# Strassen products for gate and up in the last seven weight groups of a 4-bit FFN, block sums on VectorE and GpSimd

## What is computed

```python
Wg = dequant_nvfp4(gate_W_packed, gate_scales)      # [4096, 512]
Wu = dequant_nvfp4(up_W_packed, up_scales)          # [4096, 512]
Wd = dequant_nvfp4(down_W_packed, down_scales)      # [512, 4096]
gate = jnp.einsum('th,nh->tn', xt, Wg)
up = jnp.einsum('th,nh->tn', xt, Wu)
gelu = jnp.tanh(0.7978845608028654 * (gate + 0.044715 * gate ** 3)) * gate * 0.5 + gate * 0.5
out = jnp.einsum('tn,hn->th', gelu * up, Wd)
```

## Time and profile before

| | |
|---|---|
| runs, us | 2811.38, 2810.78, 2814.67; median 2811.38 |
| profiled execution, us | 2812.82 |
| its span, us | 2811.0 |
| mean granted TensorE clock | 0.950 |
| busy over the span | TensorE 94%, VectorE 75%, GpSimd 44%, ScalarE 41% |

### The profile page before, as it was taken

How to read it: one execution, slowest core, us unless ns; L and a number is a source line. 1 busy time by engine, 2 the same in 40 slices (tenths; PEclk the granted TensorE clock), 3 DMA queues, 4 the chain that set the end, 5 groups by cost and what they waited for, 6 DMA issues and landing times.

```text
span 2811.0 us, 32430 instructions
## 1 busy us (share of the span) xinstructions
PE 2632.4 (94%) x11088; PEld 1873.9 (67%) x11096; DVE 2119.0 (75%) x2720; ACT 1150.8 (41%) x1690; POOL 1249.9 (44%) x836
## 2 busy tenths in 40 slices
PE   7888988888898879999999999999999999999999
PEld 4443444444344337888887777888878788888887
DVE  6999999999999986643366677777877865555553
ACT  5555455555545535422254442433343422222221
POOL 3989888888889871210001023223212422222220
PEclk9988898899889879999999999999999999999999
DMA  7755645555465427221111112112111111111111
GB/s 251 221 165 141 181 135 139 157 155 140 127 181 157 136 79 265 83 83 45 49 65 68 38 45 68 38 51 64 49 41 46 46 50 48 46 53 46 53 45 68
DMA packets 152309, 275.35 MB, mean 98 GB/s; under 512 B 27344, under 2 KB 27856, under 8 KB 151632
## 3 DMA queue, kind: packets, MB, share of 16 engines
q1 hardware_dynamic: 152144, 273.27, 32.8%
HBM read 178.01 MB, written 61.34 MB: 85 GB/s over the span
## 4 chain that ended last, share of the span: by engine, by line
PE 72%; DVE 11%; ACT 7%; issue 4%; POOL 3%; DMA 2%; SPq 0%; DVEq 0%; POOLq 0%; ACTq 0%
PE ps L1722 19%; PE ps L1724 19%; PE ps L1723 19%; PE ps L1763 8%; DVE state L1347 5%; ACT ps L848 5%; PE ps L1775 4%; POOL read L1173 2%; DMA vpack<-vl 1%; DMA uraw<-y_d 1%; PE ps L1914 1%; PE ps L1888 1%; DVE drive L1338 1%; POOL wdeq L1232 0%; DVE act_o L1662 0%
## 5 line engine op out<-in xcount | busy, mean ns | idle before, releaser
L1173 POOL TENSOR_TENSOR read<-state,c_t 128x512 f32<-128x512 f32 x512 | 666.8, 1315 | 121.8 <-DVE state L1347 89.1
L1347 DVE TENSOR_TENSOR_SCAN state<-ps,drive 128x512 f32<-128x512 f32 x512 | 620.4, 1212 | 15.0 <-ACT ps L848 13.3
L1232 POOL TENSOR_TENSOR wdeq<-packed,scales 128x1024 f32<-128x1024 f16 x96 | 256.1, 2668 | 799.1 <-DVE packed L1495 799.1
L1722 PE MATMUL ps<-xh,ghi 128*128 128x512 f32 x1536 | 608.0, 396 | 0.0
L1724 PE MATMUL ps<-xh,glo 128*128 128x512 f32 x1536 | 598.5, 390 | 0.0
L1723 PE MATMUL ps<-xl,ghi 128*128 128x512 f32 x1536 | 598.3, 390 | 0.0
L848 ACT ACTIVATE ps<-ps,a_exp 128x512 f32<-128x512 f32 x512 | 338.9, 662 | 470.7 <-PE ps L1763 469.5
L1763 PE MATMUL ps<-dpack,sel 128*128 128x512 f32 x512 | 259.9, 508 | 108.0 <-DVE state L1347 106.5
L1338 DVE TENSOR_TENSOR drive<-ps,b_t 128x512 f32<-128x512 f32 x512 | 342.3, 669 | 16.4 <-PE ps L1763 15.7
L1662 DVE TENSOR_TENSOR act_o<-act_o,ps 128x512 f32<-128x512 f32 x192 | 131.7, 686 | 290.5 <-PE ps L1724 288.8
L1100 ACT ACTIVATE ahi<-act_o 128x512 fp32r<-128x512 f32 x192 | 121.4, 632 | 521.5 <-DVE act_o L1662 521.4
(11 more groups left out here) (193 smaller groups left out, 3747.6 us busy)
## 6 DMA issues: line engine op xcount, KB each, us to landing
whi<-w_d SPq DMA_DIRECT2D x63, 256.0 KB, 4.1
wlo<-w_d SPq DMA_DIRECT2D x63, 256.0 KB, 5.3
b_d<-ev SPq DMA_DIRECT2D x32, 256.0 KB
dpack<-dh SPq DMA_DIRECT2D x64, 128.0 KB, 4.0
dpack<-dl SPq DMA_DIRECT2D x64, 128.0 KB, 3.8
b_t<-b_d SPq DMA_DIRECT2D x32, 256.0 KB, 4.1
vpack<-vh SPq DMA_DIRECT2D x64, 128.0 KB, 3.6
vpack<-vl SPq DMA_DIRECT2D x64, 128.0 KB, 2.8
```

The lines of the kernel that those rows point to most:

```text
L1173: pool.tensor_tensor(read[:, n % RRING, :], state[:, n % SRING, :], c_t[:, g % 2, :], ALU.mult).then_inc(read_ready, 1)
L1232: pool.tensor_tensor(wdeq[:, :].rearrange("p (h n) -> p h n", h=2), codes, scale, ALU.mult).then_inc(deq, 1)
L1347: dve.tensor_tensor_scan(state[:, n % SRING, :], ps[:, n % 2, :], drive[:, n % DRING, :], 0.0, ALU.mult, ALU.add)\
L1722: pe.matmul(out_, w_h, x_h, start=(start and k == 0), stop=False)
```

## The change

Groups 17 to 23 (`FAST_E` = 17 on) get their own loop, written over 44 units `v` a group. Each weight tile is taken as 2x2 blocks: output blocks j = 0, 1 by halves of the feature dimension (k = 0, 1 in the code's `block_`; each half has two feature tiles); the inputs of batches 2 and 3 are the 2x2 blocks of the other operand. With A the weight blocks and X the input blocks, the seven products (Winograd's form) are

```diff
+FAST_E = ALL_E - FFN_E + 1
+M1_AT, M5_AT, M6_AT, M2_AT, M7_AT, M3_AT, M4_AT = (
+    (0, 6, 13, 20), (1, 8, 15, 22), (2, 9, 16, 23), (3, 10, 17, 24), (4, 11, 18, 25),
+    (5, 12, 19, 26), (7, 14, 21, 28))
+UNITS = 44
+OUTS = ((0, 0), (0, 1), (1, 1), (1, 0))
...
+    xp = [post(f"xp{i}", [P, 2, S], F32, X0_ + 4096 * i) for i in range(4)]
+    xd = [post(f"xd{i}", [P, 2, S], F32, XL0 + 4096 * i) for i in range(4)]
+    xdlo = [post(f"xdlo{i}", [P, 2, S], F32R, XL0 + 4096 * i) for i in range(4)]
+    xdhi = [post(f"xdhi{i}", [P, 2, S], F32R, XH0 + 4096 * i) for i in range(4)]
+    act4 = [post(f"act4{o}", [P, S], F32, X0_ + 2048 * o) for o in range(4)]
+    m1_c11 = post("m1_c11", [P, S], F32, X0_ + 8192)
+    u2_c12 = post("u2_c12", [P, S], F32, X0_ + 10240)
+    m5_c22, u3_c21 = act_o
+    wsum = post("wsum", [P, 4, 2, P], F32, X0_ + 12288)
+    shi = [post(f"shi{k}", [P, 4, 2, P], F32R, 16384 * k) for k in range(2)]
+    slo = [post(f"slo{k}", [P, 4, 2, P], F32R, 16384 * k + 8192) for k in range(2)]
...
+            def store_out(b):
+                sp.wait_ge(added, 8 * (2 * MLP_E + FFN_E * (b // 2 + 1)) - 4 + 4 * (b % 2))
+                sp.dma_start(out[:, :, cols(b)], res[:, :, cols(b)]).then_inc(stored, 16)
+            for p in range(24 * FAST_E):
+                if p == 24 * FAST_E - 21:
+                    store_out(0)
+                    store_out(1)
...
+            for T in range(6 * FAST_E + 5, ALL_T):
+                load_tile(T)
+            store_out(2)
+            store_out(3)
...
+            def sum_high(q):
+                act.wait_ge(w_summed, fast1 + q + 1)
+                if q >= 2:
+                    act.wait_ge(m3_ready, fast0 + q - 1)
+                else:
+                    act.wait_ge(stored, 32)
+                act.activation(shi[q % 2][:, :, :, :], wsum[:, :, :, :], ACT.Copy, scale=UNF16)\
+                   .then_inc(s_hi, 1)
...
+            def copy_m5(q):
+                act.wait_ge(m5_ready, fast0 + q + 1)
+                taken(q - 1, 2)
+                act.activation(m5_c22[:, :], ps[:, bank_of_unit(M5_AT, q), :], ACT.Copy)\
+                   .then_inc(m5_copied, 1)
...
+                if T > 6 * FAST_E and T % 6 in (1, 2, 3, 4):
+                    pool.wait_ge(w_summed, fast1 + fast_tile(T // 6, T % 6 - 1) + 1)
...
+            def sum_weights(T):
+                q = fast_tile(T // 6, T % 6)
+                block_ = wdeq[:, :].rearrange("p (k f j n) -> p k f j n", k=2, f=2, j=2)
+                a11, a12, a21, a22 = (block_[:, k, :, j, :] for j in range(2) for k in range(2))
+                pool.wait_ge(deq, T - MLP_T + 1)
+                if q:
+                    pool.wait_ge(s_lo, fast1 + q)
+                else:
+                    pool.wait_ge(xd_ready, xd0 + 4)
+                pair_done[0] += 2
+                pool.tensor_tensor(wsum[:, 0, :, :], a21, a22, ALU.add).then_inc(pairs_summed, 1)
+                pool.wait_ge(pairs_summed, pair_done[0] - 1)
+                pool.tensor_tensor(wsum[:, 1, :, :], wsum[:, 0, :, :], a11, ALU.subtract)\
+                    .then_inc(pairs_summed, 1)
+                pool.tensor_tensor(wsum[:, 2, :, :], a11, a21, ALU.subtract)
+                pool.wait_ge(pairs_summed, pair_done[0])
+                pool.tensor_tensor(wsum[:, 3, :, :], a12, wsum[:, 1, :, :], ALU.subtract)\
+                    .then_inc(w_summed, 1)
+            def make_u4_c22(q):
+                pool.wait_ge(m5_copied, fast0 + q + 1)
+                pool.wait_ge(u3_made, fast0 + q + 1)
+                pool.tensor_tensor(u2_c12[:, :], u2_c12[:, :], m5_c22[:, :], ALU.add).then_inc(u4_made, 1)
+                pool.wait_ge(u4_made, fast0 + q + 1)
+                pool.tensor_tensor(m5_c22[:, :], u3_c21[:, :], m5_c22[:, :], ALU.add).then_inc(c22_made, 1)
...
+            def whole_input(i):
+                kk, b = ((0, 2), (0, 3), (1, 3), (1, 2))[i]
+                pool.wait_ge(n_lo, B)
+                pool.tensor_tensor(xp[i][:, :, :], xh[b][:, 2 * kk:2 * kk + 2, :].bitcast(F32),
+                                   xl[b][:, 2 * kk:2 * kk + 2, :].bitcast(F32), ALU.add)\
+                    .then_inc(xp_ready, 1)
...
+            def sum_low(q):
+                dve.wait_ge(s_hi, fast1 + q + 1)
+                dve.scalar_tensor_tensor(out=slo[q % 2][:, :, :, :], in0=wsum[:, :, :, :], scalar=UNF16,
+                                         in1=shi[q % 2][:, :, :, :].bitcast(F32), op0=ALU.mult,
+                                         op1=ALU.subtract).then_inc(s_lo, 1)
...
+            def make_c12(q):
+                dve.wait_ge(m3_ready, fast0 + q + 1)
+                dve.wait_ge(u4_made, fast0 + q + 1)
+                dve.tensor_tensor(u2_c12[:, :], u2_c12[:, :], ps[:, bank_of_unit(M3_AT, q), :], ALU.add)\
+                   .then_inc(c12_made, 1)
...
+                dve.wait_ge(act_done, first_u(q) + o + 1)
+                dve.tensor_tensor(act4[o][:, :], act4[o][:, :], up[:, :], ALU.mult).then_inc(prod_done, 1)
...
+            for E in range(FAST_E, ALL_E):
+                for v in range(UNITS):
+                    if v == 0:
+                        add_down(E - 1, 7)
+                    for k in range(4):
+                        q = fast_tile(E, k)
+                        if v == M6_AT[k] + 1:
+                            make_u2(q)
+                        if v == M2_AT[k] + 1:
+                            make_c11(q)
+                        if v == M7_AT[k] + 1:
+                            make_u3(q)
+                        if k % 2 and v == M2_AT[k] + 1:
+                            gated(q, 0)
+                        if v == M3_AT[k] + 2:
+                            make_c12(q)
+                            if k % 2:
+                                gated(q, 1)
+                        if k % 2 and v == M3_AT[k] + 3:
+                            gated(q, 2)
+                        if v == M3_AT[k] + 3:
+                            make_c21(q)
+                        if k % 2:
+                            if v == M3_AT[k] + 3:
+                                gated(q, 3)
+                            if v == M3_AT[k] + 5:
+                                a_low(q, 2)
+                                a_low(q, 3)
+                    for k in range(7):
+                        if v == (33, 34, 35, 36, 38, 40, 42)[k]:
+                            add_down(E, k)
...
+                    if v == 9:
+                        sum_low(fast_tile(E, 2))
+                    if v == 11:
+                        w_low(6 * E + 3)
+                    if v == 13:
+                        unpack(6 * E + 4)
+                    if v == 16:
+                        sum_low(fast_tile(E, 3))
+                    if v == 17:
+                        w_low(6 * E + 4)
+                    if v == 20:
+                        unpack(6 * E + 5)
...
+            def block_product(table, q, weights, inputs):
+                (w_h, w_l), (x_h, x_l) = weights, inputs
+                return three_pass(ps[:, bank_of_unit(table, q), :],
+                                  [(w_h[f], w_l[f], x_h[f], x_l[f]) for f in range(2)])
...
+            for E in range(FAST_E, ALL_E):
+                for v in range(UNITS):
+                    for k in range(4):
+                        q, T = fast_tile(E, k), 6 * E + k
+                        if v == M1_AT[k]:
+                            pe.wait_ge(w_lo, T + 1)
+                            if q == 0:
+                                pe.wait_ge(added, 8 * FAST_E)
+                            elif k == 0:
+                                pe.wait_ge(c11_made, fast0 + q)
+                            else:
+                                pe.wait_ge(u2_made, fast0 + q)
+                            block_product(M1_AT, q, weight_block(T, 0, 0), input_block(0, 2))\
+                                .then_inc(m1_ready, 1)
...
+                        if v == M6_AT[k]:
+                            if q:
+                                pe.wait_ge(c12_made, fast0 + q)
+                            block_product(M6_AT, q, sum_block(q, 1), difference_block(1))\
+                                .then_inc(m6_ready, 1)
...
+                        if v == M3_AT[k]:
+                            pe.wait_ge(m5_copied, fast0 + q + 1)
+                            block_product(M3_AT, q, sum_block(q, 3), input_block(1, 3))\
+                                .then_inc(m3_ready, 1)
+                        if v == M4_AT[k]:
+                            pe.wait_ge(c11_made, fast0 + q + 1)
+                            block_product(M4_AT, q, weight_block(T, 1, 1), difference_block(3))\
+                                .then_inc(m4_ready, 1)
...
+                    if v == 32:
+                        pe.wait_ge(a_lo, 8 * FAST_E + 4 * (E - FAST_E) + 4)
+                        pe.wait_ge(a_lo_pool, fast1 + 4 * (E - FAST_E) + 4)
+                    if 32 <= v <= 35:
+                        down_part(E, v - 32, (2, 3))
```

(3 more changed lines are left out.)

322 lines of the change are left out of this document (306 added, 16 removed).

## The result

The changed kernel takes **2903.74 us** (median of 4 runs, 2902.11 to 2905.91); the kernel before took 2812.62 us beside it. The ratio is 1.0324, 95% interval 1.0306 to 1.0342: 3.2% slower. The profiled execution took 2904.5 us, its span 2902.7, the mean granted clock was 0.940. The forecast was 2893, with a range of 2825 to 2960.

What follows compares the result with a forecast made beforehand. TensorE's instruction count was taken as the bound. Seven groups at 530.2 against 457.0 us (+73.2), group 16 +2 and the clock's 7 gave +82 on 2812.8, 2895; the median 1.4 lower: 2893 us, range 2825 to 2960.

Steps and rivals of the forecast that it cites:

- The turns: VectorE and GpSimd alternate whole instructions on SBUF work: 29.1 us a group for VectorE, 36.8 for GpSimd.
- Some 16.5 us behind GpSimd: Part of the 76.6 us group: the time VectorE's queue loses behind GpSimd's operations, about 16.5 us.
- The price without a row: GpSimd's turn for a 256-column sum, taken as 0.60 us from a line through other rows.
- The layout by hand: VectorE's and GpSimd's queues of one fast group set against each other at the turn prices: 76.6 us a group.
- Switch: Entry into the seven fast groups, where product one waits for the last add: 1.0 us.
- The clock's term: TensorE's slow restarts at 1.2 GHz after stalls in the fast groups: 1 us a group, 7 in all.
- Perfect packing: Rival: turns packed without a gap, a fast group takes 65.9 us; 2808 to 2816 us in all; 4%.
- the two faster cases: Rivals: VectorE's order alone binds, 62.6 us a group, 2794 us, 5%; all of the 38.1 us saved, 2775, 2%.
- the floor: Sum of both engines' turns in a fast group, packed without a gap: 65.9 us.
- the ceiling: VectorE's 50.9 us and all of GpSimd's 36.8 one after the other in a fast group: 87.7 us.
- The clock's rival: Stalls lower the granted clock under 0.78 and TensorE binds the fast groups again: 2950 to 3070 us; 6%.
- Three signs: Expected: VectorE busy over 90%, TensorE's longest waits also before M4 on C11, GpSimd dequantizations over 2.65 us.

Runs made afterwards that it cites:

- e8: Changed kernel with 12 unread matmuls more before product M6 of the second, third and fourth tile of a group: 2903.1 us.
- e6: Kernel before the change, with GpSimd given the change's new operations in the last seven groups, into memory nobody reads: 2814.1 us.
- e3: Changed kernel with GpSimd's weight sums cut to 8 of 256 columns from the fourth tile of group 17 on: 2885.4 us.
- e2: Changed kernel with U4, C22 and the two activation splits of a pair moved from GpSimd to VectorE: 2882.1 us.

## Why the prediction was right

**What bounds.** Right: TensorE was the bound before, and it no longer is. e8 shows the second half: with 36 matmuls more a group, groups 18 to 23 did not get longer.

**What it removes and adds.** The counts were exact. VectorE's own work was put at 50.9 us; busy 67.3 less the loss of 15.6 is 51.7.

**The turns.** The mechanism was right and e6 shows it alone. "Some 16.5 us behind GpSimd" was 15.6. The second unpack was laid out at 5.5 us and took 5.56. The price without a row, 0.60 for the turn of a 256-column sum, was right. The turn is the time from the end of VectorE's operation to the end of the sum that waited for it; in group 20 (GpSimd, VectorE, GpSimd):

```profile
2604.39 0.75 POOL L1409 TENSOR_TENSOR wsum<-wdeq 128x256 f32<-128x256 f32 x1 [1.66 <-DVE slo L1897]
...
2605.67 0.83 DVE L1971 TENSOR_TENSOR act<-act,m_c 128x512 f32<-128x512 f32 x1
...
2605.90 1.20 POOL L1413 TENSOR_TENSOR wsum<-wdeq 128x256 f32<-128x256 f32 x1
```

The multiply ends at 2606.50 and the sum at 2607.10. The 0.75 us of the first sum, which nobody held up, is its length from start to end; a turn is some 0.14 shorter. In the same way 512 columns take 1.29 alone and 1.15 as a turn, 1024 take 2.40 and 2.26. One small reading was off: the unpack of the earlier trace rows lost 3.4 us (0.37, 2.06 and 0.98), not 3.2; nothing hangs on it.

**The layout by hand.** Counted from where VectorE leaves the last unpack of the group before, M6 of tiles two, three and four were laid at 12.6, 26.6 and 41.8. In group 20 VectorE leaves it at 2588.31, and the three start at 2600.90, 2615.00 and 2630.34: 12.6, 26.7 and 42.0. From there to the next such point it took 35.7 instead of 34.8. What the layout had wrong is TensorE's place beside VectorE: its first product started 4.3 us before that point (2583.98), not 0.9. TensorE only waits longer for it at the first M6, since VectorE's queue closes the loop. One agreement in the first tile is luck. The layout left about 1.7 us before U2 (4.35 - 0.9, less 1.14 and 0.60 for the two operations between), where VectorE would wait for TensorE; there it waited for nothing, and then 2.25 us for ScalarE's part of a weight split that the layout had ready.

**The sum.** Switch, group 17 and its clock's 1 us: forecast 75.9, measured 78.0. Groups 18 to 22: 77.6 each, measured 78.1. Group 23: 73.3, measured 73.2. So 80.2 forecast, 84.8 measured. Group 16, forecast +2, was +4.8. The five PSUM banks did not cover VectorE's lateness: TensorE waited 3.1 us there for the seventh activation split (line 1996), behind an unpack and all that the group had added before it. It then restarted slowly, with matmuls 0.43 us apart for 3 us, and as TensorE still leads in that group, the other 1.7 us are the restart. With the scatter of 2.1 this is the distance of 10 us between 82 and 91.7.

**The clock's term.** The stalls do bring slow restarts (0.50 for 5 us), as "TensorE: Matmul & The Clock Gate", section "HAM oscillation — how this bites in real kernels", in the Trainium skill has it for work that comes after a long enough wait. I charged 1 us a group for them, 7 in all. e8, with the clock at 0.98 to 1.00, is 3.7 us faster in groups 18 to 23, 0.6 a group; and 1.7 fell in group 16, where I had charged none. The size was about right, its grounds were weak: I had written that TensorE had gaps of 3 to 4.5 us in the scan stage, but its longest idle time there, from 60 to 1040 us, is 1.7. The 0.4 a group that I charged too much stood in for VectorE's waits, which were 10.4 a group and not 9.

**The rivals.** Perfect packing (65.9 a group) and the two faster cases fell with the first group: 77.7 lies between the floor of 65.9 and the ceiling of 87.7, near the 76.6 of the layout. The clock's rival needed a granted clock under 0.78; it was 0.91 to 0.96 over a group, and in e8 0.98 to 1.00 with nearly the same time.

**What would show it.** C12 before M6, the slow unpacks, the untouched PSUM operations and the clock under 1 came as said. Three signs did not. VectorE was busy 87%, not over 90. C11 (line 1932) cost TensorE 6.0 us in all, four waits of 1.5 before M4, a tenth of what C12 cost. And GpSimd's dequantizations got no slower, from 2348 to 2902:

```profile
L1396 POOL TENSOR_TENSOR wdeq<-packed,scales 128x1024 f32<-128x1024 f16 x39 | 98.5, 2527 | 78.4 <-DVE packed L1738 78.4
...
L1735 DVE TENSOR_TENSOR bits_a<-bits_a,packed 128x512 int32<-128x512 int32 x39 | 51.1, 1310 | 1.3
...
L1730 DVE TENSOR_SCALAR bits_b<-bits_a 128x512 int32<-128x512 int32 x39 | 38.3, 981 | 1.3
```

2.53 us on the mean against 2.65 in the earlier trace rows. The unpack carries half of the loss: 1.31 us on the mean for the OR and 0.98 for the mask behind it, where 0.69 and 0.42 stood.

## What to carry to other kernels

Count what a saving on TensorE adds to the next engine before you count what it saves. Where VectorE and GpSimd both work from SBUF, add their times up, as their turns here had to be; VectorE's operations with one input in PSUM (0.68 us beside a busy GpSimd as alone) don't count in that sum. A change that is too large in full may pay in part: with half of the tiles VectorE's 54.1 us fit under TensorE's 62.56, where the full change put 67.3 beside 59.85. With that room, putting splits and unpacks behind the operations that TensorE waits for made TensorE dense; in the full version the moves that were tried did not. VectorE's busy share, 87% in the slow kernel and in the fast one, told nothing of that. Where a run comes out as long as another, compare the groups one by one before you call a term nothing: in e8 a gain of 3.7 us and a loss of 2.05 had all but cancelled.

## What had not been expected of the hardware

- The turns fall on the engine with the many short instructions. In e6 VectorE was busy 17.4 us a group longer over the same 61 instructions. Leaving out 97% of the columns of GpSimd's weight sums (e3) gave back 2.7 of 15.6 us, moving twelve 512-column operations (e2) 9.3.
- After an idle of 4.28 us TensorE ran about 5 us at clock 0.50, with matmuls 0.43 us apart, and in e8, where 12 matmuls shortened each gap, that stretch was at 1.00. What this costs depends on who leads: 0.6 us a group behind VectorE's queue, but 1.7 us in the one restart of group 16, after an idle of 3.14 us, where TensorE led.
- From the end of the other engine's operation to its own, an operation that waited takes some 0.14 us less than its length alone. On GpSimd 0.75, 1.29 and 2.40 us (256, 512 and 1024 columns) become 0.60, 1.15 and 2.26; on VectorE 0.42 (a mask), 0.69 and 1.22 become 0.28 to 0.34, 0.55 and 1.08. These are the values of the changed kernel from 2355 us on and of e6.
